# A vision tower on one core: roots on ScalarE, an attention loop with one more step of lag, and low halves on VectorE

## The chip, the cores and the metric

One Trainium2 chip, of which the kernel uses one core. The metric is the device time of one launch in microseconds; three timed runs of a kernel give its median. The profile is one more execution, taken by the hardware profiler.

## The reference

A tower of two layers over 16 images of 36 patches (576 tokens of 192 channels):

```python
h = tok(x)                                             # 576x768 @ 768x192, + bias
h = h + attn(layernorm(h))                             # 12 heads of 64, mask by blocks of 64 tokens
h = h + bitlinear_ffn(layernorm(h))                    # inputs rounded to 8 bit, weights to -1, 0, 1
h = h + ttt_attn(layernorm(h))                         # one gradient step of a 16x16 state per head and image
h = h + moe(layernorm(h))                              # 8 experts, top 2, capacity 180
```

In the third stage each token and head needs `1 / sqrt(var + 1e-6)` twice: once for the keys (before the gradient), once for the new state's output. With 108 rows (3 images) by 3 tiles by 12 heads that is a tile of 108x36, four times in all. An image has 36 tokens, fewer than a block of 64, so that the mask is true everywhere and attention is a softmax over the 36 tokens of an image.

## The kernel before

Every matrix product whose inputs are float32 is made of three products in float16: each operand is split into a high half (a ScalarE copy to float16) and a low half (float32 minus the high half, by VectorE or GpSimd), and high x high, high x low and low x high are summed in PSUM. The order of work on each engine is written out by hand, engine by engine, with semaphores. PSUM banks are handed out in a ring of eight by `plan`; `claim` waits until the bank's last user has emptied it.

The stages that the change touches:

- **Start.** After the token projection VectorE normalises five tiles of tokens into `xc` (L832), with the power of -0.5 from GpSimd (L1558), TensorE transposes them (L483), ScalarE makes `xnT` and its high half `x16` (L1344, L1348), VectorE the low half (L858). `w_qkv` is split in three pieces: ScalarE makes the high halves (L1337, L1339, L1350), VectorE the low half for V (L854), GpSimd those for K and Q (L1569), each 96x1536. Then TensorE makes V (L495). VectorE sums the absolute feed-forward weights (L863, L864) and makes the low halves of V (L871). V goes through DRAM and comes back laid out per pair of images (`Vbd`, 32 transfers on SyncE's queue).
- **K and Q.** For each of six pairs of heads TensorE makes K and Q in two column halves each (L513). ScalarE makes the high halves (L1366 twice per K half, L1371 once per Q half), VectorE the low halves (L901, L909). Between them VectorE rounds the feed-forward weights (L888 to L893) and ScalarE copies them to `w2q` and `wiq` (L1361, L1373). All K and Q must be evacuated before the first scores.
- **Attention loop.** Eight pairs of images, p = 0 to 7, in steps s. TensorE makes the scores S(s) (L539), then the transposes PT(s-2) of the high and low probabilities (L548), then the values PV(s-3) (L559). VectorE takes the low half of P(s-2) (L956), the row maximum and the subtraction for S(s) (L960, L963), sum and reciprocal for s-1 (L968, L971), a copy of the low PT(s-2) (L978), and the low half `aoT` of PV(s-3) (L984). ScalarE makes the exponential (L1377), the copy of the high PT (L1383), the high half of P (L1389) and of PV (L1393). GpSimd scales P by the reciprocal (L1586), and after pair 4 makes the low half of `w_out` (L1589).
- **After the loop.** VectorE runs `ttt_weights` (L915 to L938, fourteen small steps for the third stage) at s = 9, and the residual of tile 0, ahead of the low half of PV(7). The output projection (L527) of tiles 3 and 4 needs that low half.
- **Third stage.** For n = 0, 1 (three tiles each): VectorE adds the rows (`linear`, L1080), ScalarE squares (L1459), VectorE reduces (L1086, L1087), GpSimd takes the power of -0.5 of 108x36 (L1635), and VectorE makes the gradient (L1106 to L1125). TensorE makes the weight gradient (L645), VectorE the new state's weights (`w_step`, L1095), TensorE the new state's output Z (L659, L663) and the sums of its squares (L677), VectorE the variance (L1130), GpSimd the power again (L1635), VectorE spreads it (L1136) and TensorE transposes it (L685). ScalarE evacuates Z (L1469, L1470) and holds the table of the sigmoid.
- **Experts.** `expert_high` loads an expert's weights as float16, `negate_high` (ScalarE, L399, L400) writes their negative, and `expert_low` (GpSimd's queue, L405, L406) adds the float32 weights onto it. On GpSimd the low loads of experts 1 to 3 stand between the last power of 108x36 and the powers of the last layernorm (L1647).

The softmax loop's order on VectorE in the code:

```python
for s in range(PAIRS + 3):      # p = s - 2: low half of P
    ...                         # S(s): maximum, subtraction
    ...                         # p = s - 1: sum, reciprocal
    ...                         # p = s - 2: copy of the low PT
    ...                         # p = s - 3: low half of PV
```

## Time and profile before

| | us |
|---|---|
| three timed runs, median (lowest, highest) | 351.49 (348.82, 353.91) |
| profiled execution, its own time | 348.83 |
| its span, first to last instruction | 347.0 |
| busy: TensorE / VectorE / ScalarE / GpSimd | 261.6 / 210.9 / 145.5 / 112.0 |

A row of the timeline has the start in us from the first instruction, the duration of the row (from the first to the last of its instructions), engine and line, what is written and read with its shape, and how many instructions it merges. In brackets stand the idle time of the engine before the row and who ended it. PE is TensorE, DVE is VectorE, ACT is ScalarE, POOL is GpSimd. The tables by stretch give busy time with the number of instructions, and the granted clock of TensorE as a share of 2.4 GHz: 0.5 is 1.2 GHz.

### The profile page before, as it was taken

What the parts mean: (1) busy time and instruction counts of PE and PEld (TensorE: products, weight loads), DVE (VectorE), ACT (ScalarE), POOL (GpSimd) and SP (SyncE); (2) the same over time, 40 slices, a digit from 0 to 9 for tenths busy, and PEclk for the clock granted to TensorE, in tenths of its full rate; (3) what the DMA queues carried; (4) which work ended last, traced back from release to release, by engine and by line L of the source; (5) the groups of instructions that cost most, each with busy time, mean ns of one, the idle gap of its engine ahead of it and who ended that gap; (6) DMA issues with size and microseconds to landing.
All of it is one profiled execution on the core that took longest, in us unless ns stands there. A gap on an engine that the chain in (4) does not pass through costs nothing.

```text
span 347.0 us, 6603 instructions
## 1 busy us (share of the span) xinstructions
PE 261.6 (75%) x2546; PEld 220.2 (63%) x2546; DVE 210.9 (61%) x577; ACT 145.5 (42%) x291; POOL 112.0 (32%) x111
## 2 busy tenths in 40 slices
PE   3928998676658559448909869486689999999993
PEld 2713676666648424225809859475589889998883
DVE  2598699666666886974194921197336646554453
ACT  5275689244542546542724402305316335252320
POOL 7066920021421296446707060872202002010000
PEclk9965999688869855555975555585559999999998
DMA  7994432330001359560000000099501405005001
GB/s 235 295 227 118 159 70 66 71 96 2 3 2 10 60 102 205 105 68 2 1 0 2 0 0 0 3 116 155 65 5 9 63 0 63 10 3 68 1 2 51
DMA packets 17986, 21.80 MB, mean 63 GB/s; under 512 B 10019, under 2 KB 13923, under 8 KB 17731
## 3 DMA queue, kind: packets, MB, share of 16 engines
q0 software_dynamic: 4096, 9.44, 19.4%
q1 hardware_dynamic: 13859, 11.94, 12.3%
q8 instruction: 20, 0.33, 0.4%
q14 instruction: 11, 0.09, 0.1%
HBM read 28.60 MB, written 2.21 MB: 89 GB/s over the span
## 4 chain that ended last, share of the span: by engine, by line
PE 54%; DVE 23%; issue 9%; POOL 7%; ACT 4%; DMA 1%; DVEq 0%; SPq 0%; ACTq 0%; POOLq 0%
PE bank L771 10%; PE bank L749 5%; PE bank L783 5%; PE bank L495 4%; POOL arena_v L1635 4%; PE bank L513 3%; PE bank L622 3%; PE bank L796 3%; PE bank L527 3%; PE bank L468 3%; PE bank L645 2%; PE bank L755 2%; POOL arena L1586 2%; PE bank L663 2%; DVE xc L832 2%
## 5 line engine op out<-in xcount | busy, mean ns | idle before, releaser
L1635 POOL TENSOR_TENSOR arena_v<-arena_v,mhalf 108x36 f32<-108x36 f32 x4 | 24.5, 6117 | 37.5 <-DVE arena_v L1130 21.1
L405 POOL DMA_DIRECT2D arena_k<-in_w x4 | 3.4, 845 | 68.4 <-ACT arena_k L400 68.4
L1586 POOL TENSOR_TENSOR arena<-arena,ri 128x432 f32<-128x432 f32 x8 | 7.3, 911 | 48.7 <-DVE ri L971 48.7
L1558 POOL TENSOR_TENSOR rs<-arg,mhalf 128x1 f32<-128x1 f32 (+1 forms) x20 | 12.7, 670 | 28.1 <-DVE arg L827 24.4
L645 PE MATMUL bank<-arena 108*97 108x96 f32 x72 | 12.9, 374 | 9.5 <-issue 8.2
L771 PE MATMUL bank<-arena,arena_v 96*128 96x180 f16 x192 | 18.7, 265 | 1.8 <-DVE arena L1272 1.8
L771 PEld LDWEIGHTS bank<-arena,arena_v 96*128 96x128 f16 x192 | 18.0, 109 | 1.9 <-DVE arena L1272 1.9
L1271 DVE CAST arena<-arena 96x360 f16<-96x360 f32 x8 | 2.7, 344 | 26.7 <-ACT cwx L1526 26.7
L749 PE MATMUL bank<-arena 128*96 128x180 f16 (+1 forms) x160 | 18.7, 262 | 0.2 <-DVE arena L1253 0.2
L548 PE MATMUL bank<-idh,arena 128*72 128x128 f16 x96 | 9.2, 243 | 12.7 <-ACT arena L1389 6.9
L645 PEld LDWEIGHTS bank<-arena 108*97 108x97 f32 x72 | 12.2, 284 | 9.8 <-issue 8.3
L1533 ACT ACTIVATE arena<-bank 128x360 f32<-128x360 f32 x16 | 7.5, 469 | 24.8 <-PE bank L771 24.8
L513 PE MATMUL bank<-arena,arena_k 96*128 96x288 f16 x144 | 17.8, 286 | 0.0
L539 PE MATMUL bank<-arena_k,arena 128*64 128x72 f16 x288 | 14.3, 240 | 4.1 <-DVE arena L909 4.1
L796 PE MATMUL bank<-arena 90*128 90x192 f16 (+1 forms) x160 | 15.5, 247 | 1.8 <-DVE arena L1298 1.8
L539 PEld LDWEIGHTS bank<-arena_k,arena 128*64 128x64 f16 x288 | 13.5, 148 | 4.7 <-issue 4.6
L513 PEld LDWEIGHTS bank<-arena,arena_k 96*128 96x128 f16 x144 | 14.1, 98 | 3.5
L749 PEld LDWEIGHTS bank<-arena 128*96 128x96 f16 (+1 forms) x160 | 13.8, 131 | 3.8 <-issue 1.0
L548 PEld LDWEIGHTS bank<-idh,arena 128*72 128x72 f16 x96 | 6.9, 128 | 14.4 <-issue 14.2
L483 PE MATMUL bank<-idf,xc 128*96 128x128 f32 (+1 forms) x30 | 7.6, 355 | 10.8 <-DVE xc L832 10.8
L771 PE MATMUL bank<-arena,arena_k 96*128 96x180 f16 x192 | 15.7, 240 | 0.0
L468 PE MATMUL bank<-arena_v,arena 128*128 128x192 f16 (+1 forms) x90 | 10.7, 280 | 6.0 <-DVE arena_v L841 6.0
(261 smaller groups left out, 723.5 us busy)
## 6 DMA issues: line engine op xcount, KB each, us to landing
arena_v<-in_w POOLq DMA_DIRECT2D x8, 384.0 KB, 6.3
arena_k<-in_w POOLq DMA_DIRECT2D x8, 384.0 KB, 6.4
arena_v<-in_xT SPq DMA_DIRECT2D x6, 288.0 KB, 4.1
arena_v<-in_wqkv SPq DMA_DIRECT2D x3, 576.0 KB, 11.6
arena_v<-v_scratch SPq DMA_DIRECT2D x32, 54.0 KB
v_scratch<-arena SPq DMA_DIRECT2D x4, 384.0 KB, 2.3
arena_v<-in_w POOLq DMA_DIRECT2D x8, 192.0 KB, 7.4
arena_k<-in_w POOLq DMA_DIRECT2D x8, 192.0 KB, 7.4
```

What stands on the lines that cost most here:

```text
L468: ins = mm(at_bank("embed", i)[0:r, 0:D], xpT[:, a_, k, 128 * i:128 * i + r], wp16[:, w_, k, :], start=k == 0 and n == 0, stop=k == KC - 1 ...
L495: ins = mm(bk[0:r, 0:384], x16[:, a_, j, 128 * i:128 * i + r], wqkv[:, w_, j, 1536 + 384 * c:1536 + 384 * c + 384], start=n + j == 0, stop ...
L513: ins = mm(bk[:, 0:288], wqkv[:, w_, j, o + 128 * hp:o + 128 * hp + 128], x16[:, a_, j, 288 * n:288 * n + 288], start=m + j == 0, stop=m = ...
L539: ins = mm(bk[64 * x:64 * x + 64, 72 * hp:72 * hp + 72], qT[:, a_, hp, NP * b:NP * b + 64], Kbd[:, w_, hp, b, :], start=n == 0, stop=n == 2)
L548: ins = tr(bk[0:72, :].bitcast(F16)[:, 128 * hp:128 * hp + 128], P16[:, p % 2, c, 72 * hp:72 * hp + 72], idh[:])
L645: ins = mm(bk[0:HF + 1, HF * b:HF * b + HF], Km[:, G3 * t + b, j, :], GG[:, t, HF * j:HF * j + HF], start=True, stop=True)
L749: ins = mm(bk[0:HF, CAP * j:CAP * j + CAP], xsp[0:r, x, i, HF * j:HF * j + HF], oh[0:r, e % 2, i, :], start=i == 0 and x == 0, stop=i == N ...
L771: ins = mm(bk[:, CAP * m:CAP * m + CAP], w13p[e][:, wx, j, f:f + 128], zp[:, zx, j, :], start=n == 0, stop=n == 5)
L783: ins = mm(bk[0:SH, D * s:D * s + D], actp[:, ax, m, SH * s:SH * s + SH], w2p[e][:, wx, m, :], start=n == 0, stop=n == 11)
L796: ins = mm(bank[i // 2][0:r, D * (i % 2):D * (i % 2) + D], ohT[:, e % 2, s, 128 * i:128 * i + r], yp[:, x, s, :], start=False, stop=e == E ...
L1586: g.tensor_tensor(pv, pv, ri[:, p % 2, :].unsqueeze(2).broadcast_to([128, AH, NP]), ALU.mult).then_inc(normed, 1)
L1635: g.tensor_tensor(hv[1][:, o], hv[0][:, o], half_[0:TR, 0:1].broadcast_to([TR, 3 * TH]), ALU.pow).then_inc(tt_rstd, 1)
```

## The change

1. **Roots.** The four powers of 108x36 leave GpSimd. ScalarE takes the square root (`roots`), VectorE the reciprocal and one Newton step (`head_rstd`, five small instructions, each waiting for the one before). ScalarE's table goes from square root to sigmoid and back twice. The copies `negate_high` of experts 1 and 2 move one place down.
2. **Attention.** K and Q are made in two passes: columns of images 0 to 7 for all heads, then the first scores, then the second pass in steps s = 0 to 2 of the loop. TensorE makes S one step ahead, PT lags by three steps and PV by four. VectorE's order within a step becomes sum and reciprocal, maximum and subtraction, low half of P, low half of PV; the copy of the low PT goes to ScalarE. The loop has twelve steps in place of eleven. Rounding of the feed-forward weights moves into steps 3 to 5, their copies into steps 6 and 8. `ttt_weights` stands at s = 10, behind the residual of tile 0.
3. **Low halves.** VectorE makes those of K's and Q's weights (before the sums of absolute weights) and that of `w_out` (at s = 7) in place of GpSimd. The raw `w_out` is loaded over the place of `w_qkv` once the last Q has been made.
4. Rounded values of the feed-forward stage are float16 in place of bfloat16, and the bfloat16 identity is gone.

```diff
 SH = CAP // 2
+KCOLS = ((0, T // 2), (T // 2, T))
...
+            plan("k", hp, 0)
+            plan("q", hp, 0)
+        plan("S", 0)
+        for s in range(PAIRS + 4):
+            if 0 <= s - 4:
+                plan("PV", s - 4)
             if 0 <= s - 3 < PAIRS:
-                plan("PV", s - 3)
-            if s >= PAIRS:
-                plan("wo", s - PAIRS)
+                plan("PT", s - 3, 0)
+                plan("PT", s - 3, 1)
+            if s < 3:
+                for hp in (2 * s, 2 * s + 1):
+                    plan("k", hp, 1)
+                    plan("q", hp, 1)
+            if s + 1 < PAIRS:
+                plan("S", s + 1)
+            if s >= PAIRS + 1:
+                plan("wo", s - PAIRS - 1)
...
-            sp.wait_ge(wq_done, 2)
+            wait_full(sp, "q", HP - 1, 1)
             load(woraw, "woT")
...
+            scores(0)
+            for s in range(PAIRS + 4):
+                if 0 <= s - 4:
+                    values(s - 4)
+                p = s - 3
                 if 0 <= p < PAIRS:
...
+                if s < 3:
+                    for hp in (2 * s, 2 * s + 1):
+                        keys_queries(hp, 1)
+                if s + 1 < PAIRS:
+                    scores(s + 1)
+                if s >= PAIRS + 1:
+                    output_projection(s - PAIRS - 1)
...
+            for n in range(2):
+                dve.wait_ge(wqk_hi, n + 1)
+                o = slice(768 - 768 * n, 1536 - 768 * n)
+                v.tensor_tensor(wqkv[:, 1, :, o], wqkvraw[:, :, o], wqkv[:, 0, :, o], ALU.subtract).then_inc(wqk_lo, 1)
...
-            for s in range(PAIRS + 3):
-                p = s - 2
+            for s in range(PAIRS + 4):
+                p = s - 1
                 if 0 <= p < PAIRS:
+                    dve.wait_ge(exped, p + 1)
+                    st_.then(v.tensor_reduce(sm[:, p % 2, :], P[:, p % 3, :].rearrange("p (h k) -> p h k", k=NP), AX.X, ALU.add))
                     if p >= 2:
-                        wait_full(dve, "PT", p - 2, 1)
-                    dve.wait_ge(p_hi, p + 1)
-                    v.tensor_tensor(P16[:, p % 2, 1, :], P[:, p % 3, :], P16[:, p % 2, 0, :], ALU.subtract).then_inc(p_lo, 1)
+                        dve.wait_ge(normed, p - 1)
+                    v.reciprocal(ri[:, p % 2, :], sm[:, p % 2, :]).then_inc(rinved, 1)
...
+                    v.tensor_tensor(P16[:, p % 2, 1, :], P[:, p % 3, :], P16[:, p % 2, 0, :], ALU.subtract).then_inc(p_lo, 1)
+                if s < 3:
+                    for hp in (2 * s, 2 * s + 1):
+                        kq_low(hp, 1)
+                p = s - 4
...
+                if s == 3:
+                    st_.then(v.tensor_scalar(stage2[:], stage2[:], sw[:, 1:2], 1.0, ALU.mult, ALU.min))
+                    v.tensor_scalar(stage2[:], stage2[:], -1.0, MAGIC, ALU.max, ALU.add).then_inc(wq_sum, 1)
+                if s == 4:
+                    st_.then(v.tensor_scalar(stage13[:], stage13[:], sw[0:HF, 0:1], 1.0, ALU.mult, ALU.min))
+                if s == 5:
+                    v.tensor_scalar(stage13[:], stage13[:], -1.0, MAGIC, ALU.max, ALU.add).then_inc(wq_sum, 1)
+                if s == PAIRS - 1:
+                    dve.wait_ge(wo_hi, 1)
+                    v.tensor_tensor(woT[:, 1], woraw, woT[:, 0], ALU.subtract).then_inc(wo_lo, 1)
+                if s >= PAIRS + 2:
+                    residual(s - PAIRS - 2)
+                if s == PAIRS + 2:
                     ttt_weights()
...
+            def head_rstd(n, k):
+
+                a, b_, c_ = heads(hv[0], n), heads(hv[1], n), heads(hv[2], n)
+                dve.wait_ge(tt_sqrt, k)
+                st_.then(v.reciprocal(b_, b_))
+                st_.then(v.tensor_tensor(c_, b_, b_, ALU.mult))
+                st_.then(v.tensor_tensor(c_, c_, a, ALU.mult))
+                st_.then(v.tensor_scalar(c_, c_, -0.5, 1.5, ALU.mult, ALU.add))
+                st_.then(v.tensor_tensor(b_, b_, c_, ALU.mult))
...
+                kq_high(hp, 0)
+            for s in range(PAIRS + 4):
                 p = s - 2
+                if 0 <= p < PAIRS:
+                    act.wait_ge(normed, p + 1)
+                    if p >= 2:
+                        wait_full(act, "PT", p - 2, 0)
+                    a(P16[:, p % 2, 0, :], P[:, p % 3, :], ACT.Copy).then_inc(p_hi, 1)
+                p = s - 4
+                if 0 <= p:
+                    bk = wait_full(act, "PV", p)
+                    a(aoT[:, 0, :, 72 * p:72 * p + 72], bk[:, 0:432].rearrange("p (h q) -> p h q", h=HP),
+                      ACT.Copy).then_inc(ao_hi, 1)
+                p = s - 3
                 if 0 <= p < PAIRS:
                     if p >= 2:
...
+                if s < PAIRS:
+                    wait_evac(act, "S", s)
+                    a(P[:, s % 3, :], P[:, s % 3, :], ACT.Exp).then_inc(exped, 1)
                 p = s - 3
                 if 0 <= p < PAIRS:
-                    bk = wait_full(act, "PV", p)
-                    a(aoT[:, 0, :, 72 * p:72 * p + 72], bk[:, 0:432].rearrange("p (h q) -> p h q", h=HP),
-                      ACT.Copy).then_inc(ao_hi, 1)
-                if s == 4:
+                    bk = wait_full(act, "PT", p, 1)
+                    frees(a(PT[:, p % 2, 1, :], bk[0:72, :].bitcast(F16)[:, 0:768], ACT.Copy), "PT", p, 1)
+                if s < 3:
+                    for hp in (2 * s, 2 * s + 1):
+                        kq_high(hp, 1)
+                if s == 5:
                     act.wait_ge(loaded("woT"), 16)
                     a(woT[:, 0], woraw, ACT.Copy).then_inc(wo_hi, 1)
+                if s == 6:
+                    act.wait_ge(wq_sum, 1)
+                    a(w2q[:], stage2[:], ACT.Identity, bias=nmagic[:, 0:1]).then_inc(wq_done, 1)
+                if s == 8:
+                    act.wait_ge(wq_sum, 2)
+                    a(wiq[:], stage13[:], ACT.Identity, bias=nmagic[0:HF, 0:1]).then_inc(wq_done, 1)
...
+            def roots(k):
+                n = k % 2
+                if k < 2:
+                    act.wait_ge(tt_var, k + 1)
+                else:
+                    wait_evac(act, "var", n)
+                a(hv[1][:, n * 36:n * 36 + 36], hv[0][:, n * 36:n * 36 + 36], ACT.Sqrt).then_inc(tt_sqrt, 1)
+
+            table(ACT.Sqrt)
             act.wait_ge(loaded("bmask"), 16)
             z_square(0)
-            for t in range(3):
+            k_masked(0)
+            roots(0)
+            rates(0)
+            for t in range(1, 3):
                 k_masked(t)
-            rates(0)
+            table(ACT.Sqrt)
...
                 k_masked(t)
             z_square(1)
+            roots(1)
             rates(1)
-            negate_high(act, 1)
+            table(ACT.Sqrt)
             for u in range(3):
                 z_out(u)
-            negate_high(act, 2)
+            negate_high(act, 1)
+            roots(2)
             for u in range(3, TT):
                 z_out(u)
+            roots(3)
             table(ACT.Exp)
+            negate_high(act, 2)
             negate_high(act, 3)
...
-            for n in range(2):
-                pool.wait_ge(wqk_hi, n + 1)
-                o = slice(768 - 768 * n, 1536 - 768 * n)
-                g.tensor_tensor(wqkv[:, 1, :, o], wqkvraw[:, :, o], wqkv[:, 0, :, o], ALU.subtract).then_inc(wqk_lo, 1)
...
-                if p == 4:
-                    pool.wait_ge(wo_hi, 1)
-                    g.tensor_tensor(woT[:, 1], woraw, woT[:, 0], ALU.subtract).then_inc(wo_lo, 1)
...
-            def head_rstd(k):
-                o = slice(3 * TH * (k % 2), 3 * TH * (k % 2) + 3 * TH)
-                g.tensor_tensor(hv[1][:, o], hv[0][:, o], half_[0:TR, 0:1].broadcast_to([TR, 3 * TH]), ALU.pow).then_inc(tt_rstd, 1)
```

What stands on VectorE at the start, between the low half of V's weights and the sums of the absolute weights, before:

```order
L854 TENSOR_TENSOR arena_k<-arena_v,arena_k 96x2x768
L858 TENSOR_TENSOR arena<-xnT,arena 96x2x128 x4
L858 TENSOR_TENSOR arena<-xnT,arena 96x2x64
L863 TENSOR_REDUCE wsum<-stage_a 96x1
L864 TENSOR_REDUCE wsum<-stage 128x1
L871 TENSOR_TENSOR arena<-bank,arena 128x384 x8
```

and after the change:

```order
L868 TENSOR_TENSOR arena_k<-arena_v,arena_k 96x2x768
L872 TENSOR_TENSOR arena<-xnT,arena 96x2x128 x4
L872 TENSOR_TENSOR arena<-xnT,arena 96x2x64
L878 TENSOR_TENSOR arena_k<-arena_v,arena_k 96x2x768 x2
L881 TENSOR_REDUCE wsum<-stage_a 96x1
L882 TENSOR_REDUCE wsum<-stage 128x1
L889 TENSOR_TENSOR arena<-bank,arena 128x384 x8
```

Two subtractions of 96x1536 now stand in front of the sums and of V's low halves (L889).

ScalarE in one step of the attention loop (s = 6, between two exponentials), before: exponential, copy of the high PT, high half of P, high half of PV.

```order
L1377 ACTIVATE arena<-arena 128x432
L1383 ACTIVATE arena<-bank 72x768
L1389 ACTIVATE arena<-arena 128x432
L1393 ACTIVATE arena<-bank 128x6x72
L1377 ACTIVATE arena<-arena 128x432
```

After: high half of P, high half of PV, copy of the high PT, exponential, copy of the low PT; L1426 is the high half of `w_out`.

```order
L1402 ACTIVATE arena<-arena 128x432
L1406 ACTIVATE arena<-bank 128x6x72
L1413 ACTIVATE arena<-bank 72x768
L1416 ACTIVATE arena<-arena 128x432
L1420 ACTIVATE arena<-bank 72x768
L1426 ACTIVATE arena<-arena_k 128x1152
```

A fifth instruction has joined the step, and it stands behind the exponential.

ScalarE in the third stage up to the first evacuation of Z, before (L1459 square, L1453 masked keys, L1462 sigmoid, L1481 Q):

```order
L1459 ACTIVATE arena<-arena 108x576
L1453 ACTIVATE arena<-bank,bmask 108x2x96 x9
L1462 ACTIVATE arena_v<-arena 108x36
L1481 ACTIVATE arena<-bank,cols 96x288 x4
L1453 ACTIVATE arena<-bank,bmask 108x2x96 x9
L1459 ACTIVATE arena<-arena 108x576
L1462 ACTIVATE arena_v<-arena 108x36
L399 ACTIVATE arena_v<-arena_v 96x2048
```

After (L1494 square, L1488 masked keys, L1513 root, L1497 sigmoid, L1527 Q), from the first masked keys on:

```order
L1488 ACTIVATE arena<-bank,bmask 108x2x96 x3
L1513 ACTIVATE arena_v<-arena_v 108x36
L1497 ACT_TABLE_LOAD
L1497 ACTIVATE arena_v<-arena 108x36
L1488 ACTIVATE arena<-bank,bmask 108x2x96 x6
L1354 ACT_TABLE_LOAD
L1354 ACTIVATE warm<-mhalf 128x1
L1527 ACTIVATE arena<-bank,cols 96x288 x4
L1488 ACTIVATE arena<-bank,bmask 108x2x96 x9
L1494 ACTIVATE arena<-arena 108x576
L1513 ACTIVATE arena_v<-arena_v 108x36
L1497 ACT_TABLE_LOAD
```

The roots stand right behind what makes the variances, and table loads stand around them.

## Rows read from the trace of the kernel before

**Rows 1.** Busy time, granted clock and DMA share by stretch: attention, first expert, second expert.

```profile
63.26:115.20 51.94, 35.83 (x726) 33.52 (x727) 33.40 (x77) 19.41 (x33) 11.46 (x12) 0.79 0.16 36
246.45:260.25 13.80, 12.00 (x84) 10.82 (x84) 3.27 (x12) 1.94 (x7) 0.51 (x1) 0.54 0.40 44
260.25:271.30 11.05, 11.05 (x129) 10.08 (x129) 6.95 (x19) 6.42 (x12) 1.74 (x2) 1.00 0.29 31
```

**Rows 2.** Timeline from 21 to 42 us: around the low halves of `w_qkv`.

```profile
21.89 0.36 DVE L832 TENSOR_SCALAR xc<-h,mv,rs 128x192 f32<-128x192 f32 x1
22.63 3.08 POOL L1569 TENSOR_TENSOR arena_k<-arena_v,arena_k 96x1536 f16<-96x1536 f32 x1
22.69 3.14 DVE L832 TENSOR_SCALAR xc<-h,mv,rs 64x192 f32<-64x192 f32 x1 [0.44 <-POOL rs L1558]
25.76 1.74 DVE L854 TENSOR_TENSOR arena_k<-arena_v,arena_k 96x1536 f16<-96x1536 f32 x1
...
27.93 12.99 PE L495 MATMUL bank<-arena_k,arena 96*128 96x384 f16 x60 [1.54 <-DVE arena_k L854]
...
28.97 2.27 DVE L863 TENSOR_REDUCE wsum<-stage_a 96x1 f32<-96x2048 f32 x1
...
41.66 0.58 DVE L871 TENSOR_TENSOR arena<-bank,arena 64x384 f16<-64x384 f32 x1 [0.40 <-ACT arena L1355]
```

**Rows 3.** Timeline around 60 us: the last low halves of K and Q.

```profile
60.29 1.87 DVE L901 TENSOR_TENSOR arena_k<-bank,arena_k 64x288 f16<-64x288 f32 x4
62.19 0.82 DVE L909 SCALAR_TENSOR_TENSOR arena<-bank,arena 128x288 f16<-128x288 f32 x2
```

**Rows 4.** Timeline from 82 to 90 us: one step of the attention loop.

```profile
82.24 2.15 PE L539 MATMUL bank<-arena_k,arena 128*64 128x72 f16 x36
...
86.34 1.06 PE L559 MATMUL bank<-arena,arena_v 72*128 72x36 f16 x36
...
87.05 0.56 ACT L1377 ACTIVATE arena<-arena 128x432 f32<-128x432 f32 x1 [1.37 <-DVE arena L963]
...
87.52 0.79 ACT L1383 ACTIVATE arena<-bank 72x768 f16<-72x768 f16 x1
...
89.52 0.50 PE L548 MATMUL bank<-idh,arena 128*72 128x128 f16 x6 [0.94 <-ACT arena L1389]
```

**Rows 5.** Timeline from 109 to 116 us: the end of the attention loop.

```profile
109.09 0.17 DVE L915 TENSOR_REDUCE wmean<-w1s 96x2 f32<-96x32 f32 x1
...
109.30 0.17 DVE L916 TENSOR_SCALAR wmean<-wmean 96x2 f32<-96x2 f32 x1
...
110.32 0.53 ACT L1393 ACTIVATE arena<-bank 128x432 f16<-128x432 f32 x1 [1.85 <-PE bank L559]
...
114.50 0.61 DVE L984 TENSOR_TENSOR arena<-bank,arena 128x432 f16<-128x432 f32 x1
...
115.21 4.86 PE L527 MATMUL bank<-arena 128*128 128x192 f16 x36 [3.44 <-issue]
```

**Rows 6.** Timeline from 173 to 225 us: who waits for the four powers of 108x36.

```profile
173.18 0.76 DVE L1106 TENSOR_TENSOR arena<-arena,arena_v 108x576 f32<-108x576 f32 x1 [6.31 <-POOL arena_v L1635]
...
190.79 0.76 DVE L1106 TENSOR_TENSOR arena<-arena,arena_v 108x576 f32<-108x576 f32 x1
...
206.64 0.65 PE L659 MATMUL bank<-arena,bdw 97*96 97x108 f32 x2 [3.40 <-DVE arena L1095]
...
224.07 0.46 DVE L1136 COPY arena<-arena_v 108x576 f32<-108x576 f32 x1 [6.29 <-POOL arena_v L1635]
```

**Rows 7.** Timeline from 216 to 231 us: table load, negation, GpSimd's loads and next power.

```profile
216.07 1.28 ACT L1329 ACT_TABLE_LOAD   x1
...
217.60 1.91 ACT L399 ACTIVATE arena_v<-arena_v 96x2048 f16<-96x2048 f16 x1
...
226.80 2.46 POOL L406 DMA_DIRECT2D arena_v<-in_w  x1
...
229.81 0.71 POOL L1647 TENSOR_TENSOR rs<-arg,mhalf 128x2 f32<-128x2 f32 x1 [0.55 <-DVE arg L827]
```

242 lines of the change are left out of this document (89 added, 153 removed).

## The prediction, made before the changed kernel was run

> **What bounds the kernel now.** I read the chain of waits in order of time first, then the timeline where it changes engine, then busy time by stretch. No engine bounds the whole: TensorE is busy for 35.83 of the 51.94 us of attention, at 0.79 of full clock [rows 1], and three hand-overs set the pace.
>
> At the start VectorE's subtraction of 64x192 takes 3.14 us where its neighbour of 128x192 takes 0.36, beside a GpSimd subtraction of 3.08 us that began 0.06 us earlier; V's low half (25.76) and TensorE's V (27.93) queue behind it [rows 2]. Attention is a round of short steps over four engines; its last low half of PV, whose high half is ready at 110.85, starts at 114.50 because `ttt_weights` is ahead of it from 109.09, and TensorE waits 3.44 us [rows 5]. In the third stage VectorE waits 6.31 and 6.29 us for the first and last power of 108x36; the second ends just when `w_step` does, so that nothing waits for it alone; the third holds TensorE for 3.40 us by way of `w_step` [rows 6]. In the experts TensorE itself is the bound (11.05 of 11.05 us for the second [rows 1]); the change doesn't touch them.
>
> **Start.** Without GpSimd's subtraction VectorE takes 0.36 for 3.14: V's products start 2.7 us earlier, at 25.2. Little of that reaches K and Q. The low halves of `x16` end at about 28, one us ahead of the sums' start at 28.97 [rows 2]; then come two new subtractions of 1.74, sums of 2.27 and some 0.9, ten low halves of V at 0.6 (41.66 is the last of them now) and some 1.0 of small steps. 28.0 + 3.5 + 3.2 + 6.0 + 1.0 = 41.7 for the first low half of K, against 43.3 by the same steps behind 42.24: 1.6 us gained, not 2.7. TensorE (V done at 25.2 + 13.0 = 38.2) is hidden behind VectorE.
>
> **First pass of K and Q.** VectorE takes (1.87 + 0.82) / 2 = 1.35 us per head pair and half [rows 3]. Six first halves end at 41.7 + 8.1 = 49.8. The first scores start there and not at 63.26, where the stretch of [rows 1] begins. But 8.1 us of K and Q and some 3.6 us of rounding are only deferred into the loop.
>
> **Loop.** Scores at slow clock take 2.15 [rows 4], so s = 0 starts on VectorE at 52.0. In s = 0 to 2 VectorE has, besides 2.7 for two head pairs, its softmax steps at 0.6 each (1.25, 2.05 and 2.6 us), and it waits: ScalarE does the exponential first and has the first high K only some 1.5 us after the subtraction. So 5.5, 6.4 and 6.4: the second pass ends at 70.3. s = 3 takes 3.7 with the rounding.
>
> From s = 4 the circle is ScalarE and TensorE: low PT copied, values 1.06, high PV 0.5, high PT 0.79, exponential 0.56, low PT 0.79 [rows 4]: 3.7 us a step, the hand-overs set against the overlap of neighbouring rows; VectorE's 3.1 fit beside it, and TensorE's own 1.06 + 2 x 0.50 + 1.25 fit too at full clock. Extra on ScalarE: `w_out`'s high half in s = 5 (1.2), `w2q` in s = 6 (0.9), `wiq` in s = 8 (2.0). ScalarE's last row of s = 3 would end at 73.6, 0.4 ahead of VectorE's. 73.6 + 4 x 3.7 + 2.1 = 90.5; s = 8 without exponential 3.1 + 2.0 gives 95.6, s = 9 2.6, s = 10 3.3: 101.5. Values of pair 7 wait for an output projection and end at 104. VectorE meanwhile does the low half of PV(6), the residual of tile 0 and `ttt_weights` (4.3 us, from 109.09 to the 113.4 at which the residual of tile 0 follows, 1.1 ahead of 114.50), up to 106.1. It is again ahead of the last low half of PV: that ends at 106.7, and the output projection of tile 3 starts at 106.8 against 115.21 [rows 5]. **Gain 8.4 us**, the start included. `w_out`'s low half on VectorE (1.2 us at s = 7) lies in VectorE's slack. Its load is issued behind the 32 transfers of V, as now, and wanted only in s = 5.
>
> Bounds: if every TensorE part of a step takes double, it needs 2.1 + 2.0 + 2.2 = 6.3 at the worst; at full clock 3.3. I take the middle, 4.8, for that case: 1.1 us over the circle's 3.7 in each of four steps, and the gain is 4. At best VectorE doesn't wait in s = 0 to 2 (3 us less) and the gain is 11.
>
> **Roots.** A square root of 108x36 on ScalarE isn't in the trace. Its nearest rows are smaller and larger than it: an instruction of two columns is 0.17, an activation of 432 is 0.56 [rows 4, 5]; I take 0.3. Five dependent small steps are 0.21 apart, as 109.09 and 109.30 show [rows 5]: 1.05. With two hand-overs a root costs 1.55 for 6.31; were it 0.17 and five steps at 0.3, 1.9. Root 1: gain 4.75. Root 2: nothing was waited for, and its five steps now stand on VectorE behind `w_step`: loss 1.05. Root 3: TensorE's wait of 3.40 falls away but for 0.1 (gain 3.3); the next limit is its own weight gradient. Root 4: gain 4.7. Together 11.7: the row at 224.07 [rows 6] would start at 212.4.
>
> Then comes a new collision. The power at 229.81 [rows 7] follows 5.74 behind that row, so it is wanted at 218.15. Ahead of it on GpSimd stand the low loads of experts 2 and 3, which wait for ScalarE's copies. Those now come behind the last root (211.2): table 1.28 and 0.2, two times (1.91 + 0.8): 218.1. The issue of two transfers costs between 1.8 and, as at 226.80, 2 x 2.46 [rows 7]; I take 2.2. **Loss 2.2 us**, and with it **gain 9.5 us** for the stage. Behind the power queue VectorE's normalisation, the transposes and the router, so the loss passes through.
>
> The Trainium skill (SBUF — State Buffer, "SBUF: two separate sides") says that VectorE and GpSimd share a port pair which one of them locks for a whole instruction, and that descriptors of a GpSimd-issued DMA can't be written while VectorE holds it. The 3.14 us above and the growing issue rows fit it. By it the issue would stay near 2.46 each and the loss be 4.9 where VectorE is busy: 335.0 in place of 332.3.
>
> Four more table loads at 1.28 [rows 7] are on ScalarE, all before the first Z: by my times it is free at 183.2 and the first Z is there at 183.6. No loss, but no slack.
>
> The Trainium skill (ScalarE: Activation LUTs, "Table sets: the hidden batching unit") speaks against alternating sets and puts a load at about 2.7 us; the row here is 1.28. By its figure, an estimate, ScalarE would come to the first Z some 4 us late.
>
> Float16 for bfloat16 has the same width: nothing, and I see no reason for a gain or a loss.
>
> **Sum.** 348.83 (own time, span 347.0) - 8.4 - 9.5 = 330.9. That execution is as fast as the fastest of the three runs; their median is 2.66 higher. Half of that added: **332.3 us**.
>
> **Rivals.**
> - *TensorE's clock paces the loop.* For it: 0.79 in attention, with scores of 2.15 [rows 1, 4]. Against: a fuller loop has fewer gaps ahead of TensorE. Gain there 4 to 5: 336. Chance 0.15.
> - *More than forecast:* VectorE doesn't wait in the second pass and the low loads are out of GpSimd's way in time. 332.3 - 2.2 - 2 = 328. Chance 0.13.
> - *The lag gives nothing:* deferred work and `ttt_weights` use up the early scores, and only the start's 1.6 stays of 8.4. For it: all of VectorE's work remains and 3.5 us are added, and the last low half of PV is still behind `ttt_weights`. 339. Chance 0.08.
> - *The roots don't do what they say:* ScalarE is in its queue (table loads, masked keys, Q) when a variance comes, 2 to 3 us each time. Third stage gains 3: 338.5. Chance 0.05.
> - *Slower than before, by the clock of the experts:* the first expert takes 13.80 us at 0.54 and the second 11.05 at full clock [rows 1], though both have the same products; in TensorE's time it is 2.75 us or more per expert, up to the doubling of 11.05 for a whole expert at 1.2 GHz. TensorE rose after 14 us of dense work. If it stayed at 1.2 GHz for two experts more (the 19.2 us between forecast and before, by 11.05 an expert: from 1.7 experts on it is slower than before), the time would be 332.3 + 2 x 11.05 = 354.4. Nothing in the change touches that stretch. Chance 0.02.
> - My forecast: 0.57, own range 328 to 336.
>
> The range for 8 in 10 reaches from 326 to 340: the low end is gain 11 and 12, the high end the third and fourth rival. About 2% is what a measurement of this kernel tells from no change, 344.5 to 358.5. Only the slow expert clock and a mixture of two bad rivals reach it: faster 0.94, same 0.04, slower 0.02.
>
> **What would show each step.** The subtraction of 64x192 near 0.36 and V's products at 25.2; first scores at 49.8; the last second-pass low half at 70.3; ScalarE's rows from 74 to 90 without long idle, 4 us per exponential; the low half of PV(7) still behind `ttt_weights`, the output projection at 106.8. In the third stage about 1.6 us from variance to use, the second root's five steps visible behind `w_step`, TensorE going from weight gradient to new state without the wait of 3.40, and an idle VectorE of some 2 us ahead of the last layernorm's first normalisation, ended by GpSimd. I am wrong if exponentials come over 5 us apart, if the projection starts after 110, or if any root takes over 3 us.

## The result: 322.65 us, below the range of the prediction

The changed kernel took 322.65 us (median of 5 executions, 320.94 to 327.30) against 350.06 us before on the same chip: a ratio of 0.922 (0.919 to 0.926). The forecast of 332.3 us had the direction and the order of size; the time is 9.65 us below it and 3.35 us below the low end of 326. Over the study the same kernel ran 16 times, 320.9 to 330.9 us with a median of 324.8, and the longer executions have the lower mean granted clocks (0.782 to 0.795 above 326 us, 0.795 to 0.820 below 324). So these five were a little lucky: by the median of all 16 the miss is 7.5 us and the time still lies below the range. The kernel before stayed within 347.7 and 354.0. Ratios leave out executions over 1.5% above the fastest of the same kernel, and where too few are left there is a dash.

The profiled execution took 327.3 us (span 325.5), the before's 348.83. Its row of granted clock in 40 slices, and the same by stretches of the third stage (update of the weights 166 to 199.5, last normalisation and router to 225, first expert to 238.8):

```profile
PEclk9966997967869776556975555555589999999998
```

```profile
147.50:166.00 18.50, 15.24 (x102) 12.24 (x102) 12.37 (x25) 11.56 (x30) 2.96 (x10) 0.86 0.00 1
166.00:199.50 33.50, 30.48 (x184) 30.17 (x183) 17.41 (x42) 10.30 (x22) 1.76 (x2) 0.50 0.16 19
199.50:225.00 25.50, 20.25 (x97) 16.67 (x97) 20.65 (x98) 14.74 (x24) 9.90 (x15) 0.50 0.54 69
225.00:238.80 13.80, 12.00 (x84) 10.81 (x84) 3.29 (x12) 1.83 (x6) 0.26 (x1) 0.53 0.39 44
```

In this table the clock is the third figure from the end; behind the stretch's length stand the busy times of TensorE, its weight load, VectorE, ScalarE and GpSimd. TensorE is busy for 30.48 of 33.50 us in the update, all of it at the lower level. The first expert is what it was in [rows 1].

The start, timeline of the changed kernel (start, duration, engine, line, what; in brackets the wait and its end):

```profile
22.22 0.37 DVE L846 TENSOR_SCALAR xc<-h,mv,rs 64x192 f32<-64x192 f32 x1 [0.44 <-POOL rs L1608]
22.52 1.74 DVE L868 TENSOR_TENSOR arena_k<-arena_v,arena_k 96x1536 f16<-96x1536 f32 x1
...
24.69 12.47 PE L499 MATMUL bank<-arena_k,arena 96*128 96x384 f16 x60 [1.53 <-DVE arena_k L868]
...
26.55 3.42 DVE L878 TENSOR_TENSOR arena_k<-arena_v,arena_k 96x1536 f16<-96x1536 f32 x2
...
30.03 10.34 POOL L1619 MEMSET arena_v<- 72x12288 f32 x1 [7.84 <-DVE arena_k L878]
...
38.77 1.62 DVE L900 TENSOR_SCALAR mwd<-mw 128x2 f32<-128x2 f32 x1
...
40.42 0.92 DVE L906 TENSOR_TENSOR arena_k<-bank,arena_k 64x288 f16<-64x288 f32 x2
```

The subtraction of 64x192 is at 0.37 for 3.14 [rows 2] and V's products at 24.69 for 27.93. The end of attention:

```profile
48.86 1.23 PE L544 MATMUL bank<-arena_k,arena 128*64 128x72 f16 x36 [1.91 <-DVE arena L913]
...
50.20 0.61 DVE L970 TENSOR_REDUCE mx<-bank 128x12 f32<-128x432 f32 x1 [1.59 <-PE bank L544]
```

```profile
98.44 1.05 PE L556 MATMUL bank<-arena,arena_v 72*128 72x36 f16 x36
98.77 0.18 DVE L924 TENSOR_REDUCE wmean<-w1s 96x2 f32<-96x32 f32 x1
...
103.12 0.61 DVE L989 TENSOR_TENSOR arena<-bank,arena 128x432 f16<-128x432 f32 x1
103.83 1.38 PE L529 MATMUL bank<-arena 128*128 128x192 f16 x13 [2.85 <-issue]
```

The first scores start at 48.86 for 63.26, and the output projection of tile 3 at 103.83 for 115.21 [rows 5]: 11.4 us. The last low half of PV is still behind `ttt_weights`, whose first row is that at 98.77. In the third stage, the first root and the last:

```profile
155.31 0.18 DVE L1102 TENSOR_SCALAR arena_v<-arena_v 108x36 f32<-108x36 f32 x1
155.53 0.23 ACT L1513 ACTIVATE arena_v<-arena_v 108x36 f32<-108x36 f32 x1
155.78 1.28 ACT L1497 ACT_TABLE_LOAD   x1
155.80 0.38 DVE L1108 RECIPROCAL arena_v<-arena_v 108x36 f32<-108x36 f32 x1 [0.30 <-ACT arena_v L1513]
156.21 0.20 DVE L1109 TENSOR_TENSOR arena_v<-arena_v 108x36 f32<-108x36 f32 x1
...
157.08 0.23 ACT L1497 ACTIVATE arena_v<-arena 108x36 f32<-108x36 f32 x1
157.12 0.76 DVE L1131 TENSOR_TENSOR arena<-arena,arena_v 108x576 f32<-108x576 f32 x1
```

```profile
184.25 4.23 PE L659 MATMUL bank<-arena 108*97 108x96 f32 x24 [2.65 <-DVE arena L1150]
188.28 0.57 PE L673 MATMUL bank<-arena,bdw 97*96 97x108 f32 x2
```

From the variance's end (155.49) to use (157.12) a root is 1.63 us for the 6.31 of [rows 6], and TensorE goes from the weight gradient (to 188.3) straight to the new state. The last root's use is at 200.97 for 224.07. The normalisation behind it meets the collision:

```profile
206.62 0.81 POOL L409 DMA_DIRECT2D arena_v<-in_w  x1 [0.81 <-ACT arena_v L404]
207.15 1.19 POOL L410 DMA_DIRECT2D arena_v<-in_w  x1
208.41 1.40 POOL L1675 TENSOR_TENSOR rs<-arg,mhalf 128x2 f32<-128x2 f32 x2
...
209.17 0.38 DVE L846 TENSOR_SCALAR xc<-h,mv,rs 128x192 f32<-128x192 f32 x1 [1.36 <-POOL rs L1675]
```

From the third stage's first product to the first expert's first large product it is 77.6 us (147.3 to 224.9) for 87.5 (158.9 to 246.4).

### The profile page after: what moved, and what is told of

Its sections match the earlier page's. It is cut to its first block, busy times and chain, and to the rows that moved or that the text cites. A ratio compares the mean times of both kernels' runs of the same rounds, so it can differ in the third digit from the quotient of the medians.

```text
span 325.5 us, 6620 instructions
## 1 busy us (share of the span) xinstructions
PE 259.9 (80%) x2546; PEld 218.6 (67%) x2546; DVE 213.3 (66%) x591; ACT 156.3 (48%) x309; POOL 79.0 (24%) x104
## 4 chain that ended last, share of the span: by engine, by line
PE 56%; DVE 23%; issue 6%; ACT 6%; POOL 2%; DVEq 0%; ACTq 0%
PE bank L785 10%; PE bank L763 6%; PE bank L797 5%; PE bank L499 4%; PE bank L810 4%; PE bank L529 3%; PE bank L659 3%; DVE arena_k L906 2%; PE bank L556 2%; PE bank L708 2%; PE bank L769 2%; PE bank L515 2%; PE bank L636 2%; PE bank L677 2%; PE bank L544 2%
## 5 line engine op out<-in xcount | busy, mean ns | idle before, releaser
L515 PE MATMUL bank<-arena,arena_k 96*128 96x288 f16 (+2 forms) x144 | 20.0, 302 | 0.0
L785 PEld LDWEIGHTS bank<-arena,arena_v 96*128 96x128 f16 x192 | 18.1, 109 | 1.9 <-DVE arena L1297 1.9
L515 PEld LDWEIGHTS bank<-arena,arena_k 96*128 96x128 f16 x144 | 14.6, 103 | 4.5
L763 PEld LDWEIGHTS bank<-arena 128*96 128x96 f16 (+1 forms) x160 | 13.8, 130 | 3.8 <-issue 1.0
L409 POOL DMA_DIRECT2D arena_v<-in_w x4 | 3.3, 832 | 52.6 <-ACT arena_v L404 52.6
L544 PE MATMUL bank<-arena_k,arena 128*64 128x72 f16 x288 | 11.8, 213 | 5.1 <-DVE arena L913 5.1
L659 PEld LDWEIGHTS bank<-arena 108*97 108x97 f32 x72 | 11.5, 270 | 5.9 <-issue 3.2
L544 PEld LDWEIGHTS bank<-arena_k,arena 128*64 128x64 f16 x288 | 10.8, 125 | 6.5 <-issue 6.3
L810 PEld LDWEIGHTS bank<-arena 90*128 90x128 f16 (+1 forms) x160 | 13.0, 100 | 3.3 <-DVE arena L1323 2.0
L785 PEld LDWEIGHTS bank<-arena,arena_k 96*128 96x128 f16 x192 | 15.2, 97 | 0.0
L1575 ACT ACTIVATE arena<-bank,nw 96x180 f32<-96x180 f32 x16 | 5.6, 401 | 19.6 <-PE bank L769 19.6
## 6 DMA issues: line engine op xcount, KB each, us to landing
arena_v<-in_wqkv SPq DMA_DIRECT2D x3, 576.0 KB, 10.1
```

What stands on the lines that cost most here:

```text
L515: ins = mm(bk[:, 0:c1 - c0], wqkv[:, w_, j, o + 128 * hp:o + 128 * hp + 128], x16[:, a_, j, c0:c1], start=m + j == 0, stop=m == 2 and j == 1)
L544: ins = mm(bk[64 * x:64 * x + 64, 72 * hp:72 * hp + 72], qT[:, a_, hp, NP * b:NP * b + 64], Kbd[:, w_, hp, b, :], start=n == 0, stop=n == 2)
L659: ins = mm(bk[0:HF + 1, HF * b:HF * b + HF], Km[:, G3 * t + b, j, :], GG[:, t, HF * j:HF * j + HF], start=True, stop=True)
L763: ins = mm(bk[0:HF, CAP * j:CAP * j + CAP], xsp[0:r, x, i, HF * j:HF * j + HF], oh[0:r, e % 2, i, :], start=i == 0 and x == 0, stop=i == N ...
L785: ins = mm(bk[:, CAP * m:CAP * m + CAP], w13p[e][:, wx, j, f:f + 128], zp[:, zx, j, :], start=n == 0, stop=n == 5)
L810: ins = mm(bank[i // 2][0:r, D * (i % 2):D * (i % 2) + D], ohT[:, e % 2, s, 128 * i:128 * i + r], yp[:, x, s, :], start=False, stop=e == E ...
```

## The experiments

Points of the trace, in us; "stage" is the third stage's first product, "expert" the first large product of the first expert. The last column is the mean granted clock of the profiled execution; ratios are to executions of the kernel before on the same chip.

| kernel | median (range, n) | ratio | stage | expert | stage to expert | clock |
|---|---|---|---|---|---|---|
| before | 350.06 (348.4 to 353.9, 5) | - | 158.9 | 246.4 | 87.5 | 0.770 |
| changed | 322.65 (320.9 to 327.3, 5) | 0.922 | 147.3 | 224.9 | 77.6 | 0.782 |
| changed, second copy | 324.94 (321.2 to 330.6, 4) | 0.923 | 147.7 | 225.6 | 77.9 | 0.795 |
| roots only | 332.14 (331.7 to 337.9, 4) | 0.951 | 159.5 | 229.8 | 70.3 | 0.805 |
| low halves only | 347.09 (345.7 to 349.8, 10) | 0.996 | 158.5 | 246.4 | 88.0 | 0.793 |
| attention only | 340.02 (339.8 to 340.1, 4) | 0.974 | 150.7 | 238.6 | 87.9 | 0.793 |
| changed, 28 + 28 products | 321.83 (320.1 to 324.3, 5) | 0.921 | 148.1 | 219.8 | 71.7 | 0.814 |
| before, 64 + 40 products | 347.01 (344.2 to 349.7, 11) | 0.991 | 158.5 | 246.1 | 87.6 | 0.785 |
| low loads last | 325.36 (320.7 to 329.2, 5) | 0.924 | 148.0 | 225.3 | 77.3 | 0.782 |
| weights later | 329.19 (321.4 to 330.8, 5) | - | 149.1 | 227.0 | 77.9 | 0.783 |
| lag only | 323.30 (316.9 to 324.7, 5) | - | 144.8 | 222.7 | 77.9 | 0.799 |
| all waits filled | 318.19 (317.3 to 320.2, 5) | 0.912 | 148.4 | 216.9 | 68.5 | 0.865 |
| root's steps earlier | 325.64 (322.9 to 327.8, 5) | 0.927 | 148.9 | 225.5 | 76.6 | 0.781 |
| combined | 315.69 (312.7 to 316.6, 5) | 0.902 | 147.9 | 216.1 | 68.2 | 0.861 |
| combined, lag only | 310.62 (308.8 to 311.5, 5) | 0.890 | 145.0 | 209.9 | 64.9 | 0.870 |
| lag only, rounding back | 321.74 (317.7 to 327.4, 5) | 0.914 | 147.8 | 220.3 | 72.5 | 0.799 |
| waits filled, no roots | 328.25 (327.1 to 328.9, 5) | 0.941 | 147.1 | 228.0 | 80.9 | 0.879 |
| roots only, again | 334.03 (334.0 to 334.1, 2) | 0.957 | 159.1 | 231.8 | 72.7 | 0.786 |

### Part by part

The first four: the changed kernel again, and the kernel before with one part of the change each (the hunks of the diff for that part and no others; the low half of `w_out` and float16 for bfloat16 go with the attention, so that the low halves by themselves are those of K's and Q's weights).

> The changed kernel once more, nothing altered. Its first profile had a span of 325.5 us at a mean granted clock of 0.782, while three of its five runs had 319 to 321 us at 0.81 to 0.82. Theory A (the six microseconds between the two traces' difference of 21.5 us and the medians' 27.4 us are TensorE's granted clock, not instructions): a profile at 0.81 or more spans 319 to 321 us, its attention ends within 0.5 us of the first profile's (output projection's tile 3 at 103.8), and the difference lies in one or two stretches in which the granted clock is 1.0 in place of 0.5. Theory B (the times of waits differ between executions): the six microseconds are spread over all stages and the clock of each 25 us stretch agrees within 0.03. Ratio to the kernel before 0.917 to 0.928 by both.

> The kernel before with only the third stage's four square roots moved to ScalarE and VectorE; attention and the start as before. By the prediction: 11.7 us off the chain to the second root of the updated states, 2.2 us given back on GpSimd, so 9.5 us, a ratio of 0.973 (340.6 us). By the trace of the changed kernel (the stage from the third stage's first product to the first expert is 77.57 us for 87.55): 10.0 us, 0.971. Theory A (clock) lets the ratio fall to 0.95 if the shorter stage also lifts the granted clock; rival: roots gain only what the table loads leave, ratio above 0.985.

> The kernel before with only the low halves of w_k and w_q taken from GpSimd to VectorE. By the prediction the two subtractions of 64x192 go from 3.14 to about 0.36 us and the products of V follow (start 25.2 for 27.93), while VectorE, which is full there, gives back all but 1.6 us of the 2.7: a ratio of 0.995 (348.4 us). Rival (the start passes on whole): 2.7 to 3.2 us, 0.991. Rival (nothing, since the first low halves wait for the cleared arena of keys on GpSimd): 1.000.

> The kernel before with the lagged attention and with K and Q in two halves, and float16 for bfloat16; roots and the low halves of w_k and w_q as before. By the prediction the attention's gain without the start's 1.6 us: 8.4 - 1.6 = 6.8 us, 0.981 (343.3 us). By the trace of the changed kernel (output projection's tile 3 at 103.83 for 115.21, 11.4 us, less the start's 1.6 to 2.7): 8.7 to 9.8 us, 0.973. If the three parts add up (9.5 to 10.0 + 1.6 to 2.7 + 8.7 to 9.8) they give 20 to 22.5 us and not the 27.4 of the medians; the rest is then something that only the parts together bring, or each part brings more than its trace says.

The second copy of the changed kernel had a span of 324.5 us at a clock of 0.795, near that of the first trace, so neither of its two theories was decided. By medians, attention gives 9.1 us (8.7 to 9.8 by the trace of the changed kernel, 6.8 by the prediction), the low halves 1.6 (interval 0.4 to 2.7; 1.6 by the prediction) and the roots 17.3 (15.4 to 19.2) for 9.5 forecast. The large miss is that of the roots.

That these three add up to 28.0, with 27.4 for the whole, doesn't show that the parts are independent, for the traces divide the gain otherwise. The third stage starts 0.4 us earlier with the low halves alone, 8.2 with attention alone, and 10.9 to 11.6 in the four copies of the changed kernel, so 2 to 3 us come only with both. With the low halves alone VectorE's cast of the bfloat16 identity ends only at 42.29, with GpSimd's clearing (31.87 + 10.34 = 42.21), and the first low K comes at 42.81 for 43.27 before. In the changed kernel that cast is gone.

One half of a new state (two products, then six) with the roots only, and in a second copy of that kernel:

```profile
181.40 0.41 PE L659 MATMUL bank<-arena,bdw 97*96 97x108 f32 x2 [0.19 <-DVE arena L1105]
181.64 0.62 PE L663 MATMUL bank<-arena 97*96 97x36 f32 x6
```

```profile
181.63 0.60 PE L659 MATMUL bank<-arena,bdw 97*96 97x108 f32 x2
182.02 1.07 PE L663 MATMUL bank<-arena 97*96 97x36 f32 x6
```

The same six products are 0.62 us in one execution and 1.07 in the other. By stretches, the update and what follows it, first copy and second:

```profile
177.50:203.90 26.40, 20.11 (x185) 19.80 (x185) 17.79 (x42) 10.19 (x21) 1.76 (x2) 0.74 0.20 23
203.90:229.80 25.90, 16.82 (x100) 14.12 (x100) 20.71 (x99) 14.73 (x24) 9.87 (x15) 0.66 0.54 69
```

```profile
177.50:204.00 26.50, 23.73 (x164) 23.66 (x165) 18.02 (x42) 9.03 (x17) 1.76 (x2) 0.57 0.20 23
204.00:231.00 27.00, 19.93 (x118) 16.70 (x117) 20.20 (x96) 15.48 (x26) 9.12 (x15) 0.62 0.51 66
```

At 0.74 the last new state starts at 202.4, at 0.57 at 204.4, with the same wait of 3.03 us ahead of the first gradient, and stage to expert is 70.3 and 72.7 us. In the changed kernel, whose third stage has the same instructions, it is 77.6 with the update at 0.50. So 7.3 us between 70.3 and 77.6 go with the clock. Between the kernel before and the changed one, both at 0.50 in the update in their traces, it is 87.55 for 77.57: the roots are worth 10.0 us there.

The shorter chain is not what brings the upper level. With the low halves alone and with attention alone, GpSimd's powers are still there, and the first half of the update goes at the upper level all the same. With attention alone:

```profile
178.14 0.62 PE L677 MATMUL bank<-arena 97*96 97x36 f32 x6
...
191.45 3.93 PE L659 MATMUL bank<-arena 108*97 108x96 f32 x24 [7.06 <-DVE arena L1136]
```

The level gives nothing there: TensorE then waits 7.06 us for the gradient, and stage to expert is 88.0 and 87.9 us, as it is with the update at 0.50. What the roots change is that TensorE's products come to stand in the chain, and their level with them. What decides the level in an execution is not shown by these runs. The second copies:

> The kernel before with the roots alone once more. Three of its four runs had 332 us at 0.805, one 337.9 at 0.778. Theory A: a trace near 332 us has the update (177.5 to 204 us) at 0.74 as the first one; a trace near 338 us has it at 0.50 to 0.55, the gain then 11 us and not 17. Rival: the slower execution loses its 6 us elsewhere.

It came out between the two levels that it names (334.0 us, clock 0.57).

> The changed kernel once more, beside the others on the same chip: its runs so far spread from 320.9 to 330.6 us. Theory: again 321 to 330, most at 321 to 327, and the lag only 2 to 3 us below it in like executions. Ratio 0.920 to 0.930.

326.07 us (322.0 to 330.9), 0.925. The span of its trace is 324.3, the update at 0.52.

> The changed kernel a fourth time, for its trace alone: all three so far (spans 325.5, 324.5, 324.3) had the update of the weights from 166 to 199.5 us at a mean granted clock of 0.50 to 0.53. Theory A: a trace with a span near 320 us has that stretch at 0.7 or more and its last new state before 194 us, everything up to 166 us as in the others. Rival: it gains in the experts or in the attention. If the span is again over 324 us, this tells nothing new.

Two executions, 328.0 and 322.4 us; the trace has the first, with a span of 326.2 and the update at 0.51. No trace of the changed kernel shows an execution near 321 us, so where the shorter executions gain is not shown directly.

### The clock by itself

Products of 128x128 whose results are overwritten, ahead of the waits for the gradients:

```diff
             def weight_gradient(t):
+                bk = claim(pe, "gW", t, 0)
+                for _ in range({0: 28, 3: 28}.get(t, 0)):
+                    mm(bk[:, 0:128], idh[:], idh[:], start=True, stop=True)
                 pe.wait_ge(tt_g, t // 3 + 1)
...
```

> The changed kernel with 28 products of 128x128 more on TensorE ahead of each of its two waits for the gradients of the third stage (3.03 and 2.65 us idle, products of 128 columns last about 0.11 us at the lower level); their results are overwritten. Nothing else waits for them. Theory A (what the first trace lacks against the roots alone is the granted clock: the 12.9 us of new states there are the same instructions as 9.9 us in the run with the roots alone, 0.65 us a state product at 0.50 and 0.41 us at 1.0): TensorE keeps or regains the upper level through the stage, its second half (second gradient to the first product of the projection, 19.5 us) becomes 14 to 15 us, the whole stage 5 to 7 us shorter, ratio to the kernel before 0.905 to 0.912 and no more runs of 325 us. Rival (the clock follows something else, the products only sit in idle time): times and clock as of the changed kernel, ratio 0.92. Rival (they hold TensorE up at the lower level, when a wait is shorter than they are): 1 to 2 us slower, 0.925.

> The kernel before with 64 and 40 such products ahead of its two waits for the gradients (7.2 us and up to 6 us idle). Theory A: the granted clock of the stage from 181 to 227 us, 0.50 throughout, rises to 0.8 or more, while the waits for GpSimd's powers stay; the new states and the products after them give back 4 to 7 us: ratio 0.98 to 0.99. Rival (no effect of filling): 1.00. Rival (products in the way): 1.005.

```profile
182.09 3.15 PE L656 MATMUL bank<-idh 128*128 128x128 f16 x28
185.03 3.46 PE L662 MATMUL bank<-arena 108*97 108x96 f32 x24
188.32 0.35 PE L676 MATMUL bank<-arena,bdw 97*96 97x108 f32 x2
188.51 0.62 PE L680 MATMUL bank<-arena 97*96 97x36 f32 x6
```

In the changed kernel with them (above) the second wait is full, and the fourth gradient takes 3.46 for 4.23 us and the new states behind it go at the upper level. Stage to expert is 71.7 for 77.6 to 78.0: 5.9 to 6.3 us, as theory A had it, with no useful work changed. The first filling, 1.73 us in a wait of 3.03, left 1.31 idle, and the level was lost soon after. All five executions lie at 320.1 to 324.3. The ratio of 0.921 missed the 0.905 to 0.912 of theory A: the median gains less than the trace, for the changed kernel has good executions by itself. The kernel before gained 3.2 us (0.987 to 0.995), at the small end of its expectation. Its trace doesn't show where: the update stayed at 0.50 up to 200 us and rose to 0.70 only behind that, and stage to expert is 87.6 us for 87.5 without the products.

Next, products in all larger waits of TensorE, in the way of the diff above, and the same kernel with the powers back on GpSimd:

> The changed kernel with more idle time of TensorE filled by products of 128x128 whose results are overwritten: 100 ahead of the gated layer's first transposition, 48 and 28 ahead of the two gradients, 8 ahead of each transposition of the last normalisation, 24 ahead of the counts, 20 ahead of the first expert's positions and 16 ahead of its up products. Theory A (the granted clock falls after such waits and products behind them cost twice): the first expert goes from 13.9 to about 11 us, the two halves of the update go at 1.0 (the first from 18.8 to 14 us), and the gated layer's 12 us at 0.5 from 115 to 127 lose 2 to 4 us unless VectorE sets them: 7 to 12 us off the changed kernel's slower profile of 325.5, a median of 314 to 318 us, ratio 0.90 to 0.91. Rival (only the second half of the update can be gained, as in the run with 28 and 28): 0.920. Rival (the products hold up what follows them where the clock is at 0.5): 0.925 to 0.93.

> The changed kernel with GpSimd's four powers back in the third stage, and TensorE's waits filled as in the run with all waits filled (there at the places and in the lengths that its waits have: 120 products ahead of the first gradient, 12 ahead of the fourth, 55 ahead of the fourth new state, 85 to 90 ahead of the second spread). Both kernels then have TensorE mostly at 1.0, so their difference is the price of the roots at one clock. Theory A (17.3 us for the roots alone are 9.5 to 10 us of chain and 7 of clock): 9.5 to 12 us above the run with all waits filled (318.2), 328 to 330 us, 0.94. Rival (the roots themselves are worth 17 us): 335 us, 0.96. Rival (with the clock held, some of the chain hides behind other work): below 326 us.

With all waits filled the median is 318.19 and the spread 2.9 us in place of 10. With GpSimd's powers back in that same kernel it is 328.25. **With the waits filled in both, the medians differ by 10.1 us**; 9.5 was forecast. The mean clocks are near each other (0.865 and 0.879) but not level by level: without the roots, the later new states of the update's first half fall back to 1.07 us for six products, where they stay at 0.62 with them, and the first expert's first products take 2.12 for 3.69 us. Between the two traces the spans differ by 8.9 us and stage to expert by 12.4. So the 10.1 stands beside the 10.0 that the two kernels themselves show at the lower level, and the rest of the 17.3, some 7 us, is clock.

One thing with all waits filled did not turn out as expected:

```profile
115.00:127.00 12.00, 7.47 (x42) 3.68 (x42) 8.69 (x28) 8.08 (x20) 10.56 (x16) 0.92 1.01 180
```

This is the gated layer, at 0.92 for 0.50, TensorE busy for 7.47 us where the second copy of the changed kernel had 11.70. But the third stage starts at 148.4 for 147.7: nothing came of it. The chain of that copy from 115 us to the third stage lies mostly on VectorE.

### Single steps of the prediction

The low loads of experts 2 and 3 behind the last powers:

```diff
-            expert_low(pool, 2)
-            expert_low(pool, 3)
             for i in range(NT):
...
+            expert_low(pool, 2)
+            expert_low(pool, 3)
             expert_high(pool, E - 1)
```

> The changed kernel with the low-half loads of experts 2 and 3 issued on GpSimd behind the last normalisation's powers instead of ahead of them. By the prediction the collision costs 2.2 us; by the trace VectorE waits 1.36 us for that power and GpSimd waited 0.81 us for the negation within: 1.4 to 2.2 us faster than the changed kernel, 0.916 to 0.919. Rival (experts 2 and 3 come late then): not before expert 2 at 250 us, so nothing. Rival (the gain ends in another wait of the expert stage, the way to the first expert's product being bound elsewhere): 0.923.

```profile
211.29 0.14 POOL L1676 MEMSET arena<- 128x40 f32 x1 [2.00 <-PE bank L708]
...
211.58 1.35 POOL L1673 TENSOR_TENSOR rs<-arg,mhalf 128x2 f32<-128x2 f32 x2
...
212.32 0.38 DVE L846 TENSOR_SCALAR xc<-h,mv,rs 128x192 f32<-128x192 f32 x1 [1.03 <-POOL rs L1673]
```

The wait of 1.36 us went and one of 1.03 took its place: GpSimd now stood at a clearing that waits for the projection's last product, ahead of the third power. Stage to expert is 77.3 us for 77.6 to 78.0, not 1.4 less, and the ratio 0.924, as the last rival had it.

`ttt_weights()` moved from the end of the attention loop to step 1 of the gated layer's loop:

> The changed kernel with the third stage's weight preparation (4.3 us of VectorE, ahead of the last low half of the attention) moved into the gated layer's loop, where VectorE is 75% busy. Theory (VectorE's chain sets the attention's end and the normalisation behind it): TensorE's wait of 2.85 us ahead of the output projection's tile 3 goes, the normalisation comes 4.3 us earlier, 2 to 4 us faster than the changed kernel: 0.912 to 0.918. Rival (VectorE sets the gated layer too, the 4.3 us are only moved): 0.923. Rival (the TensorE clock falls with more waiting there): above 0.925.

```profile
105.24 0.95 DVE L846 TENSOR_SCALAR xc<-h,mv,rs 128x192 f32<-128x192 f32 x3
...
111.64 1.13 ACT L1442 ACTIVATE arena<-xc,nmagic 128x192 f16<-128x192 f32 x3
```

Against the second copy the normalisation came 2.3 us earlier (105.24 for 107.58) and the quantised values 2.1 (111.64 for 113.74), and the third stage began 1.4 us later. So the theory failed, and the first rival fits the trace: VectorE sets the gated layer too. The rival of a falling clock isn't excluded: four of five executions took 328.9 us or more at mean clocks of 0.776 to 0.783, the fifth 321.4 at 0.809. In the trace stage to expert is 77.8 us as in the changed kernel, so it doesn't show where they lose more than the 1.4.

Both passes of K and Q ahead of the loop, the lag kept:

```diff
-            for hp in range(HP):
-                keys_queries(hp, 0)
+            for n in range(2):
+                for hp in range(HP):
+                    keys_queries(hp, n)
...
-                if s < 3:
-                    for hp in (2 * s, 2 * s + 1):
-                        keys_queries(hp, 1)
```

> The changed kernel with the second halves of K and Q taken in front of the loop again, behind the first halves; the lag of one more step in the loop stays. By the trace of the changed kernel the first pass takes 9.4 us of TensorE and the three steps that hold the second one take 6.0 us each for about 4.0 of the later ones. Theory (halves give what the second pass costs ahead of the loop less what it costs in it): 9.4 - 3 x 2.0 = 3.4 us slower than the changed kernel, ratio 0.931. Rival (the loop's ScalarE would have been the bound in those steps, the second pass is nearly free there): 6 us slower, 0.939. Rival (the halves give nothing, all of the attention's gain is the lag): 0.922.

```profile
56.65 4.15 PE L544 MATMUL bank<-arena_k,arena 128*64 128x72 f16 x144
...
59.87 0.56 ACT L1412 ACTIVATE arena<-arena 128x432 f32<-128x432 f32 x1 [2.54 <-DVE arena L971]
...
62.47 0.56 ACT L1412 ACTIVATE arena<-arena 128x432 f32<-128x432 f32 x1 [2.03 <-DVE arena L971]
...
65.06 0.56 ACT L1412 ACTIVATE arena<-arena 128x432 f32<-128x432 f32 x1 [1.58 <-DVE arena L971]
```

By the trace all three fell; the median, 0.927 of that of the kernel before, lies between the first and the third and decides nothing. The first scores come 7.8 us later, but the first exponentials then are 2.6 us apart, not 6.0, and the third stage starts 2.5 to 3.2 us earlier than in the four copies of the changed kernel (2.9 against the second). Splitting K and Q cost 2.9 us. The expectation had compared with the later steps of 4.0 us and missed that the first steps have no products of P yet.

The same, with VectorE's rounding back among the K and Q tiles, and ScalarE's two operations likewise:

```diff
             for n in range(2):
                 for hp in range(HP):
+                    if (n, hp) == (0, 4):
+                        st_.then(v.tensor_scalar(stage2[:], stage2[:], sw[:, 1:2], 1.0, ALU.mult, ALU.min))
...
                     kq_low(hp, n)
```

> The run with the lag only (second halves ahead of the loop), with the rounding of the gated layer's weights back among the K and Q tiles, as in the kernel before: VectorE's four operations (0.62, 0.56, 1.27 and about 1.3 us) at the same three places and ScalarE's two (0.8 and 2.0 us), the last between the tiles and the loop. Theory (the prediction left out that this rounding leaves the way to the first scores, it counted it at nothing): VectorE takes 1.35 us a half tile pair, ScalarE's next one comes every 1.4 us, so 3 to 4 us later first scores (56.7 becomes 60), of which the loop gives back 1 to 2 us: 2 to 3 us slower than the lag only, 0.927 to 0.934. Rival (the lag alone makes the gain): as the lag only, 0.922 to 0.925.

The maxima of the first scores moved from 58.60 to 62.21 and the stage's start from 144.8 to 147.8: by the trace 3.0 us, as in the theory. The median says otherwise (321.74 for 323.30) because the second half of the update went at the upper level in its profile (last new state at 192.9 for 193.9, though all before the update was 3 us later). Medians that the clock moves by 10 us don't resolve 3; points of the trace ahead of the update do.

VectorE's steps of the second root ahead of the third update (and `gradient(1)` without them):

```diff
-            for t in range(3):
+            for t in range(2):
                 w_step(t)
+            head_rstd(1, 2)
+            w_step(2)
             gradient(1)
```

> The changed kernel with VectorE's five steps of the second keys' root ahead of the third update of the weights, not behind it (by the prediction this place costs 1.05 us). Theory: TensorE's wait of 2.65 us ahead of the fourth gradient shrinks by 1.3 us, 1.3 us faster: 0.919. Rival (the third update, now 1.3 us later, holds up the new state and the gradients' buffer): nothing, 0.923. The spread of the changed kernel's own runs (320.9 to 330.6 us) is larger than either, so the verdict goes by the trace: distance from the third stage's first product to the fourth gradient, 36.95 us before this edit, 35.6 by the theory.

```profile
184.86 4.23 PE L659 MATMUL bank<-arena 108*97 108x96 f32 x24 [1.32 <-DVE arena L1151]
```

The wait fell from 2.65 to 1.32 and the distance from the third stage's first product from 36.9 us (37.3 in two of the four copies) to 36.0: 1.0 to 1.3 us, which bears out the second root's loss of 1.05.

Then all of these in one kernel, with the filled waits, first without the lag only and then with it; new in it is the place of the clearing on GpSimd:

```diff
-                if i == 1:
+                if i == NT - 1:
                     wait_full(pool, "proj", NT - 1)
```

> The run before the last with three edits more: the root's steps earlier, the low loads of experts 2 and 3 behind the last powers, and GpSimd's clearing of two small tiles, which waits for the last product of the projection, behind all powers instead of after the second (with the loads alone moved, that clearing had taken the collision's place: VectorE then waited 1.03 and 0.59 us). Theory: 1.3 + 1.4 to 2 us off the run with the filled waits: 0.89 to 0.90. Rival (moved waits turn up elsewhere): as that run. This is the version meant to beat both kernels.

315.69 us, 0.902: 2.5 us below the filled waits (0.9115), for the 2.7 to 3.3 that the moves were put at.

> The combined version with the second halves of K and Q ahead of the loop as in the run with the lag only. There the output projection started 2.9 us earlier than in the changed kernel (90.3 for 93.2) and the third stage too (144.8 for 147.7). Theory (the halves cost 2.9 us by themselves, whatever the clock): 2.9 us off the combined version's 315.7, a median of 312 to 313.5, ratio 0.893 to 0.897. Rival (the 2.9 us were won by the order only where TensorE's clock happened to be high): 315 to 316, 0.903.

```profile
216.10:220.80 4.70, 3.89 (x46) 3.20 (x46) 0.90 (x3) 0.86 (x4) 0.43 (x1) 1.00 1.07 178
220.80:226.50 5.70, 5.67 (x68) 5.31 (x69) 2.80 (x11) 2.01 (x4) 0.00 (x0) 1.00 0.82 110
```

In the combined version the first expert (stretches of it above) goes at 1.0: 8.9 us from its first large product at 216.14 to the second expert's at 225.08, for the 13.8 of [rows 1]. With the lag only it reached **310.62 us, 0.890 (0.885 to 0.895)**, faster than both kernels. That is 5.1 us below the combined version for 2.9 expected: the third stage starts 2.9 us earlier, as expected, and the rest lies between stage and expert (64.9 for 68.2). Its products without use are part of the gain.

## Why the prediction was wrong

The forecast's own sum was for one execution, 348.83 - 8.4 - 9.5 = 330.9; the profiled one of the changed kernel took 327.3. That is 3.6 us: attention 3.0 and the third stage 0.5. The median lay 4.65 us below that execution, where the prediction had put it 1.33 above: 6.0 us more. Both make the 9.65. The 6.0 are put down to the clock; by the median of all 16 executions they are 3.8.

- **"TensorE rose after 14 us of dense work" was used for the experts alone.** This is the step that failed: the sum took every TensorE duration of the third stage as it was in the trace of before, and the clock came in only as a danger. The roots alone gave 17.3 us. At the lower level they are worth 10.0 (87.55 to 77.57), near the 9.5 of the sum; the other 7.3 (77.57 to 70.31) are the same products at a higher clock. As long as GpSimd's powers set the update, the level gave nothing (87.55 us at 0.50, 87.9 and 88.0 with its first half at the upper level); with the powers gone the products stand in the chain. The state products can be 0.41 or 0.65 us, and which it is varies between executions of one program. That the shorter executions of the changed kernel have the upper level in the update is inferred from the other kernels and from clock and time going together in 16 executions; none was traced.
- **Roots, 1.55 us each:** 1.63 measured. The four together gained as worked out (11.7 in the sum; stage 158.9 to the row at 224.07 was 65.2 and is 53.7, 11.5), with root 2's loss of about 1.0 in it.
- **The two figures by the Trainium skill:** by the one (SBUF — State Buffer, "SBUF: two separate sides"), the issues would have stayed near 2.46 us with a loss of 4.9; they took 0.81 and 1.19. By the other (ScalarE: Activation LUTs, "Table sets: the hidden batching unit") a table load is about 2.7 us. The rows of the loads are 1.28, as before, and behind the first root only 1.32 us pass from its end (155.76) to the sigmoid (157.08). Neither loss came.
- **The collision, loss 2.2:** it exists, 1.36 us at VectorE. The two issues of an expert took 1.7 us together (206.62 to 208.34), not 2.2. But it was no price of its own: with the loads away, the clearing behind the projection costs nearly as much.
- **Start, V at 25.2 and first low K at 41.7:** 24.69 and 40.42. The way was other than told: VectorE was done with V's low halves by 38.5 and then held by GpSimd's clearing. On its own the part gave 1.6 us by medians, the figure of the prediction, but only 0.4 at the third stage in its trace, where the clearing held VectorE to 42.2; the agreement says little.
- **First scores 49.8, VectorE at 52.0:** 48.86 and 50.20. The scores were taken at the slow clock, 2.15; they took 1.23.
- **Second pass ends 70.3:** 68.3. The three steps were put at 18.3 us together and took 18.1.
- **Loop and `ttt_weights` to 106.1:** 103.1, 1.0 us less than the prediction from 68.3 on. Exponentials came 3.6 to 4.4 us apart for 3.7 plus extras. The sum of attention, 11.4 for 8.4, is made of these. What stood in no step: the halves cost 2.9 us, the moved rounding gave 3.0, and low halves and attention together give 2 to 3 us more than singly. The rest, most of the gain, falls to the lag and the new order in the loop; that is what is left over, and no run has them alone.
- **Rivals:** "more than forecast" at 328 was the nearest, for other reasons. Neither the clock of the loop nor ScalarE's queue came true; the table loads of 1.28 us stood behind the square roots and cost nothing. The range erred by taking the clock as something that could only hurt.

## What to carry to other kernels

Where TensorE runs at the lower level through a stage and is busy there, a wait that is shortened can pay twice: once in the chain, and once because the products then stand in the chain, so that a higher level, where an execution has it, counts (here 10.0 us and up to 7.3 more). Ask for both ends of each TensorE duration, from stretches at either level, and ask who sets the stage, since a higher clock gave nothing where VectorE did. Splitting work to start a loop early is worth only what the loop's first steps have room for: here they were the lightest, and filling them cost more than it won. A sum of single gains that agrees with the whole is no proof that they add up; points of the traces can divide it otherwise. With a spread of 3% from the clock, compare points of the traces ahead of it, or hold the clock level first and then compare.

## What the runs showed of the hardware that was not expected

- The same program went through the same products in 0.62 or 1.07 us, and the changed kernel's time varied by 10 us, where the kernel before varied by 6. Filling TensorE's idle time with useless products lifted the mean clock of the trace from 0.78 or 0.80 to 0.865, and five executions then lay within 2.9 us.
- VectorE's multiplication on 128x2 elements (the row of 1.62 us at 38.77) ended only with GpSimd's clearing of 72x12288 (38.77 + 1.62 = 40.39, 30.03 + 10.34 = 40.37). In the other three copies and with the lag only, the same operation took 1.04 to 2.35 us and ended within 0.03 us of the clearing; in the kernel before, behind the clearing, it took 0.26. While the clearing ran, VectorE's reads of PSUM for V's low halves went on at 0.5 us each. The Trainium skill (SBUF — State Buffer, "SBUF: two separate sides") has a port pair that the two engines share and that one of them holds for a whole instruction; these rows agree.
- The first four scores of the changed kernel went at 1.23 to 1.25 us for 36 products, and the next, at 68.52 behind the second pass, at 2.12 for the same 36.
